# Issuing the K, V and G mixing products together in three row groups, with a new order on every engine, in an attention and mixture-of-experts kernel

## The reference, cut to what matters

```python
shifted = jnp.pad(h, ((0, 0), (1, 0), (0, 0)))[:, :T_]
delta = shifted - h
x1 = jnp.tanh(x0).reshape(B_, T_, 5, R)              # R = 32
x2 = jnp.einsum('btnr,hnr->btnh', x1, x_out_w.reshape(H_, 5, R))
mus = x2 + x_bias
r_mu, w_mu, k_mu, v_mu, g_mu = (mus[:, :, i] for i in range(5))
...
k = (h + delta * k_mu) @ k_w.T
v = (h + delta * v_mu) @ v_w.T
g = (h + delta * g_mu) @ g_w.T
```

## Time and profile before

| | us |
|---|---|
| median of 3 executions | 884.71 (884.67 to 891.51) |
| profiled execution, its own time | 889.28 |
| its span in the trace | 887.3 |
| TensorE busy in the span | 788.1 (89%) |
| GpSimd busy | 552.4 (62%) |
| ScalarE busy | 484.1 (55%) |
| VectorE busy | 471.9 (53%) |

### The profile page before, as it was taken

How to read it: one execution, slowest core, us unless ns; L and a number is a source line. 1 busy time by engine, 2 the same in 40 slices (tenths; PEclk the granted TensorE clock), 3 DMA queues, 4 the chain that set the end, 5 groups by cost and what they waited for, 6 DMA issues and landing times.

```text
span 887.3 us, 24076 instructions
## 1 busy us (share of the span) xinstructions
PE 788.1 (89%) x8042; PEld 569.7 (64%) x8043; DVE 471.9 (53%) x1381; ACT 484.1 (55%) x1147; POOL 552.4 (62%) x691
## 2 busy tenths in 40 slices
PE   4788899999999999999977759999999999999492
PEld 1354455555665656555555449999999999988340
DVE  2435877777777777687754523333333333223076
ACT  2344666656656656566643306666666666546247
POOL 5435678878887888788876634555555555455344
PEclk9977999999999999999999969999999999999796
DMA  4000112202221122211113521222222222222394
GB/s 165 13 26 2 44 54 64 64 24 62 57 67 43 43 59 63 61 41 48 47 41 91 210 69 45 73 71 67 72 70 65 66 66 62 63 61 52 113 314 142
DMA packets 70324, 63.44 MB, mean 71 GB/s; under 512 B 8002, under 2 KB 61640, under 8 KB 70112
## 3 DMA queue, kind: packets, MB, share of 16 engines
q1 hardware_dynamic: 60816, 44.99, 17.9%
q0 software_dynamic: 9152, 17.07, 5.9%
q10 hardware_dynamic: 272, 0.26, 0.1%
HBM read 38.75 MB, written 25.50 MB: 72 GB/s over the span
## 4 chain that ended last, share of the span: by engine, by line
PE 72%; POOL 8%; issue 7%; DVE 4%; ACT 3%; DMA 2%; another core or an unknown queue 2%; SPq 0%; POOLq 0%; ACTq 0%; DVEq 0%
PE psO L616 16%; PE psB L605 15%; PE psO L541 6%; PE psP L332 5%; PE psB L485 4%; POOL w_ring L939 3%; PE psB L443 3%; POOL dispatched_rows L959 3%; PE psP L407 2%; PE psP L323 2%; PE psO L548 2%; PE psP L596 2%; PE psB L475 2%; PE psP L347 2%
## 5 line engine op out<-in xcount | busy, mean ns | idle before, releaser
L982 POOL DMA_INDIRECT expert_results<-yw_all,rows x158 | 155.5, 984 | 155.8 <-ACT yw_all L857 126.9
L616 PEld LDWEIGHTS psO<-w_sb,hide 128*128 128x128 f32 x1264 | 152.9, 192 | 6.7 <-issue 2.9
L616 PE MATMUL psO<-w_sb,hide 128*128 x1264 | 154.5, 275 | 1.0 <-ACT hide L849 1.0
L849 ACT ACTIVATE hide<-psB,w_ring 128x256 f32<-128x256 f32 x316 | 123.8, 475 | 56.0 <-PE psB L605 53.8
L959 POOL DMA_INDIRECT dispatched_rows<-rows,slot x128 | 130.8, 1022 | 35.0 <-issue 31.0
L605 PE MATMUL psB<-x1T,w_ring 128*128 128x256 f32 x632 | 151.3, 383 | 0.6 <-DVE x1T L1283 0.3
L1296 DVE TENSOR_TENSOR K<-psO,b_sb 128x256 f32<-128x256 f32 x79 | 33.6, 425 | 171.4 <-PE psO L616 138.2
L605 PEld LDWEIGHTS psB<-x1T,w_ring 128*128 128x128 f32 x632 | 114.9, 192 | 14.4 <-issue 1.7
L939 POOL TENSOR_TENSOR w_ring<-w_ring,tot 128x128 f32<-128x128 f32 (+2 forms) x160 | 117.9, 759 | 0.0
L857 ACT ACTIVATE yw_all<-K,rows 128x128 f32<-128x128 f32 x158 | 54.8, 395 | 78.5 <-issue 47.1
L1034 DVE SCALAR_TENSOR_TENSOR psP<-psP,cols,delta 128x512 f32<-128x512 f32 x80 | 57.3, 754 | 72.2 <-PE psP L332 72.2
(11 more groups left out here) (172 smaller groups left out, 1302.0 us busy)
## 6 DMA issues: line engine op xcount, KB each, us to landing
rows<-dispatched_rows SPq DMA_DIRECT2D x80, 132.0 KB
w_sb<-expert_results SPq DMA_DIRECT2D x8, 1024.0 KB, 11.9
h_res<-in_hidden SPq DMA_DIRECT2D x16, 256.0 KB, 3.0
out<-w_sb SPq DMA_DIRECT2D x16, 256.0 KB, 2.3
hT<-in_hidden_t SPq DMA_DIRECT2D x15, 256.0 KB, 4.5
w_sb<-in_w SPq DMA_DIRECT2D x14, 256.0 KB
expert_results<-yw_all,rows POOLq DMA_INDIRECT x158
dispatched_rows<-pad_rows SPq DMA_DIRECT2D x17, 132.0 KB
```

The lines of the kernel that those rows point to most:

```text
L616: last = mm(psO[:, p, s * 128:(s + 1) * 128], hide[p][:, c, s * 128:(s + 1) * 128], w2_sb[:, bass.ds(e, 1), c, :].rearrange("p e c -> p (e ...
L849: last = A(hide[p][:, c, :], psB[:, 2 * p + c // 2, (c % 2) * ST:(c % 2 + 1) * ST], ACT.Relu, bias=w1b[i % W_RING][:, HIDDEN + c:HIDDEN + ...
L982: G.indirect_dma_start(back_dram[:, :], bass.IndirectOffsetOnAxis(row_in[i][:, s, AT_DEST:AT_DEST + 1].bitcast(u32), 0), yw[i][:, s, :], N ...
```

## The change

Mixture G's product goes from its own place behind `a_k` to the group of K and V. The three are then issued one after another in row groups 2, 3 and 0, into banks P0, P1 and O1, in place of P0 and P1 with G following in P1 once V's mixture had been read. As O1 is the shared expert's bank, two waits are added: the group waits for `base_out` of the unit four back, and `f_up` 0 waits for `mixed4` (G's mixture) of the unit three ahead. `a_g` now waits for `mixed3` as well, since it writes P1 where V's mixture was. The numbers of products, vector operations and DMAs stay as they were. The order tables of all four engines are new, and the pipeline runs one step more, because the tables count from another unit.

```diff
-MIX_BANK = {MIX_W: 0, MIX_R: 1, MIX_K: 0, MIX_V: 1, MIX_G: 1}
+        mix_in = {MIX_W: P0, MIX_R: P1, MIX_K: P0, MIX_V: P1, MIX_G: O1}
...
-            def a_mix_k_v(u):
+            def a_mix_k_v_g(u):
                 done(pe, "exp_w", u)
                 done(pe, "r_done", u)
-                pe.nop(nofuse=True)
-                mix(P0, MIX_K)
-                mix(P1, MIX_V)
+                before(pe, "base_out", u, 4)
+                pe.nop(nofuse=True)
+                for n in (MIX_K, MIX_V, MIX_G):
+                    mix(mix_in[n], n)
...
-            def a_mix_g(u):
-                done(pe, f"mixed{MIX_V}", u)
-                mix(P1, MIX_G)
...
             def a_g(u):
+                done(pe, f"mixed{MIX_V}", u)
                 done(pe, f"mixed{MIX_G}", u)
...
                     done(pe, "x1T", u)
                     before(pe, "base_out", u)
+                    done(pe, f"mixed{MIX_G}", min(u + 3, UNITS - 1))
...
-                at(2, b_k_tok)
-                at(3, a_mix_k_v)
-                at(2, b_kv)
...
+                at(-1, b_k_tok)
+                at(-2, c_attn)
+                at(0, a_k)
+                at(-1, b_kv)
+                at(-3, f_up, 0)
+                at(0, a_g)
+                at(-1, b_o_far)
+                at(0, a_v)
```

More of the change, by code:

```diff
@@ L218, in pipeline @@
         def pipeline(body):
-            for i in range(-4, UNITS + 3):
+            for i in range(-4, UNITS + 4):
                 def at(d, op, *args):
@@ L367, in a_mix_w_r @@
                 pe.nop(nofuse=True)
-                mix(P0, MIX_W)
-                mix(P1, MIX_R)
+                mix(mix_in[MIX_W], MIX_W)
+                mix(mix_in[MIX_R], MIX_R)
             def a_decay_hid(u):
@@ L553, in body @@
             def body(at):
-                at(0, f_up, 0)
-                at(2, b_o_near)
-                at(2, b_k_tok)
-                at(3, a_mix_k_v)
-                at(2, b_kv)
-                at(0, f_up, 1)
-                at(0, c_place)
-                at(3, a_k)
-                at(3, a_mix_g)
-                at(3, a_v)
-                at(0, f_up, 2)
-                at(2, b_o_far)
-                at(3, a_g)
-                at(1, c_attn)
-                at(3, b_level, 1)
-                at(3, b_level, 0)
-                at(4, a_adapt0)
-                at(0, f_up, 3)
-                at(4, a_adapt1)
-                at(3, b_level, 2)
-                at(0, f_down, 0)
-                at(4, a_mix_w_r)
-                at(3, b_level, 3)
-                at(0, f_down, 1)
-                at(1, c_turn)
-                at(4, a_decay_hid)
-                at(4, a_r)
-                at(1, c_logits)
-                at(3, b_level, 4)
-                at(4, a_w)
+                at(-1, b_o_near)
+                at(-1, b_k_tok)
[6 more added lines that the diff above has]
+                at(0, a_v)
+                at(0, b_level, 1)
+                at(1, a_adapt0)
+                at(-3, f_up, 1)
+                at(0, b_level, 0)
+                at(1, a_adapt1)
+                at(-3, f_up, 2)
+                at(-2, c_turn)
+                at(0, b_level, 2)
+                at(1, a_mix_w_r)
+                at(-3, f_up, 3)
+                at(-2, c_logits)
+                at(0, b_level, 3)
+                at(-3, f_down, 0)
+                at(1, a_decay_hid)
+                at(1, a_r)
+                at(-3, f_down, 1)
+                at(1, a_w)
+                at(-2, c_place)
+                at(0, b_level, 4)
+                at(1, a_mix_k_v_g)
             pipeline(body)
@@ L814, in body @@
             def body(at):
-                at(0, b_o)
-                at(1, a_g)
-                at(1, a_v)
-                at(2, a_adapt0)
-                at(-2, f_hid, 3)
-                at(2, a_adapt1a)
-                at(2, a_adapt1b)
-                at(-1, c_x1)
-                at(0, c_sq)
-                at(-1, c_x1T)
-                at(2, a_decay_hid)
-                at(-1, c_logits)
-                at(2, a_r)
-                at(2, a_w)
-                at(-1, f_hid, 0)
-                at(1, b_k_tok)
-                at(1, b_chunk_decay)
-                at(2, a_r_near)
-                at(-1, f_hid, 1)
-                at(2, a_k)
-                at(-1, c_rows1)
-                at(2, a_k_near)
-                at(2, a_decay)
-                at(-1, c_top_exp)
-                at(0, c_aff)
-                at(-1, f_hid, 2)
+                at(3, a_decay)
+                at(0, f_hid, 0)
+                at(3, a_g)
+                at(2, b_o)
+                at(2, c_sq)
+                at(3, a_v)
+                at(4, a_adapt0)
+                at(0, f_hid, 1)
+                at(1, c_x1)
+                at(4, a_adapt1b)
+                at(4, a_adapt1a)
+                at(0, f_hid, 2)
+                at(1, c_x1T)
+                at(0, f_hid, 3)
+                at(1, c_logits)
+                at(4, a_decay_hid)
+                at(4, a_r)
+                at(1, c_top_exp)
+                at(4, a_w)
+                at(2, c_aff)
+                at(3, b_k_tok)
+                at(4, a_r_near)
+                at(3, b_chunk_decay)
+                at(4, a_k)
+                at(1, c_rows1)
+                at(4, a_k_near)
             pipeline(body)
```

90 lines of the change are left out of this document (45 added, 45 removed).

## The result

| | before | after |
|---|---|---|
| median, same chip | 888.11 us (884.67 to 892.12, 4 runs) | 991.81 us (984.03 to 998.2, 4 runs) |
| profiled execution | 889.28 us | 992.62 us |
| from one `b_o_far` to the next, mean of 11 units | 28.4 us | 35.4 us |

The kernel became slower by a factor of 1.116 (95% interval 1.106 to 1.126), 104 us. The forecast was 896 us, with a range to 906.

What follows compares the result with a forecast made beforehand. TensorE was taken as the bound (busy 27.06 of 28.40 us), GpSimd second. Cycle 27.6, with late signals 28.6, plus clock falls 0.6: 29.2 us, +0.9; twelve units add 11 to 884.7, giving 896 us, range 871 to 906.

Steps and rivals of the forecast that it cites:

- Three row groups side by side: TensorE's mixing products K, V, G run together, saving 1.06 us a unit; the rival that they don't had chance 0.03.
- The new wait in front of `a_g`: TensorE waits for V's mixture, now last on VectorE: `a_g` starts 5.4 us after `b_k_tok`, idle 1.4 us every unit.
- The cycle: Way from `b_k_tok` through `a_g`, the levels and GpSimd's steps to the next `b_k_tok`: 27.6 us with signals on time.
- GpSimd's 27.0 us: GpSimd's list without its waits for TensorE, claimed as the floor no unit can go below: about 27.0 us.
- Late signals: TensorE's signals beside GpSimd's scatters arrive about 1.2 us late, lengthening the unit from 27.6 to 28.6 us.
- only `b_kv` late: Case where only `b_kv`'s signal is late: the scan starts at 4.2 instead of 3.4 us, the unit takes 28.4 us.
- The clock: TensorE's clock falls to half behind the hole before `a_g` in one of two units: 0.57 us a unit.
- never less: Claim that more TensorE idle time in one piece makes clock falls more frequent, never less; bounds one in three and each.
- Signals on time: Rival, chance 0.25: lateness belongs to the old order's place, not the scatters; unit 28.0 to 28.2 us, 881 to 883 us.
- Every unit slowed: Rival, chance 0.12: K's signal late (28.8 us) and a clock fall in each unit: 29.9 us, 904 up to 908 us.
- GpSimd becomes the bound: Rival, chance 0.20: pieces overlap better, the unit drops to GpSimd's 27.0 us, kernel faster at 869 or 873 us.
- The rest: Other new waits (`base_out`, `mixed4`), the long power, SP's queue, the first stage's start and end, later stages: all cost nothing.

Runs made afterwards that it cites:

- no scatters: Changed kernel with GpSimd's 128 indirect scatters replaced by memsets of about equal length, routed rows not dispatched: 877.35 us on A, 882.04 us on B.
- A: Not a run: the chips on which the kernel before took 885 to 888 us (chips 2 and 4 by the numbers on record).
- the old order without scatters: Kernel before the change with the same memsets in place of the scatters, routed rows not dispatched: 851.37 and 849.69 us on B.
- V first: Changed kernel with V's mixture on VectorE moved ahead of G's, `c_z` and the scan: 909.94 us (1.026) on A, 868.88 us (1.011) on B.
- B: Not a run: the chips on which the kernel before took 859 to 862 us (chips 0 and 5 by the numbers on record).
- scan behind V with one pair moved: Changed kernel with VectorE order K, G, V, `c_z`, scan, and the last scatter pair put behind `b_step` 0: 878.74 us (1.019) on B.
- one pair moved: Changed kernel with the last of GpSimd's scatter pairs put behind `b_step` 0: 937.44 us (1.058) on A, 890.27 us (1.033) on B.
- K first: V first, and on TensorE `a_k` and `b_kv` put ahead of `c_attn`: 930.77 us (1.047) on A.
- the two VectorE orders: Changed kernel with V's mixture ahead of `c_z` and the scan, before G's (909.94 us, 1.026) or behind G's (925.51 us, 1.044), on A.
- `f_up` 0 three times: Changed kernel with the products of `f_up` 0 issued three times into the same bank, as useless work in the hole: 975.16 us (1.100) on A.

## Why the prediction was wrong, step by step

The direction was right and the size was off by 96 us. My cycle has four pieces, and the runs measured each, once without late signals and once with:

| piece | my sum, on time | no scatters, A | after, A |
|---|---|---|---|
| `b_k_tok` to `a_g` | 5.4 | 5.43 | 8.30 |
| `a_g` to `b_level` 1 | 3.64 | 3.83 | 7.14 |
| `b_level` 1 to `b_level` 2 | 5.98 | 5.91 | 6.48 |
| `b_level` 2 to the next `b_k_tok` | 12.6 | 12.33 | 13.41 |
| unit | 27.6 | 27.50 | 35.33 |

**Three row groups side by side: right.** Three products take 1.14 us. The Trainium skill ("TensorE: Matmul & The Clock Gate", section on why this matters for kernels) gave a speedup of 3.07 for four, from which I had estimated up to 1.46 us; the trace is better than that. With or without the grouping the time is the same within 1%.

**The new wait in front of `a_g`: right in place, kind and on-time size.** I had 5.4 us and a hole of 1.4; without scatters it was 5.43 and 1.30.

**The cycle: right in size, partly by luck.** 27.6 against 27.50. But my last piece went through GpSimd's list and counted two holes of 0.68 us behind scatters as if they belonged to signals on time. They were late signals already. Without scatters they are gone, and GpSimd waits for TensorE's `b_level` 4 (0.89 us) instead; 12.6 against 12.33 came out of two errors that cancel. For the same reason GpSimd's 27.0 us was no floor: the old order without scatters took 26.2 us a unit, and V first 27.4 on B.

**What I compared it with: wrong.** I set 27.6, with signals on time, against 27.96, where they were late. With signals on time on both sides it is 27.5 against 26.2: the new wait costs 1.3 us a unit even then, which with a later start is the 31 us of the two kernels without scatters.

**Late signals: the step that failed.** I took 28.6, 1.0 us above the cycle, from the one late signal I had followed, K's (1.2 us), and added it at whichever product stood beside the scatters. K's was now 0.2 us late and `b_kv`'s 3.1. Even for "only `b_kv` late" I let the scan start at 4.2 us behind `b_k_tok`; it started at 6.1 (323.10 - 317.02). `a_g` starts at 8.30: +1.9 us over the 6.4 that is in the forecast of 28.6 (with K late by the full 1.2 it would have been 6.6). `b_level` 3's and 4's signals are late beside their pairs as well: 13.41 against 12.6, +0.8.

**The clock: the term that was mis-sized with it.** I allowed 0.57 us a unit, one fall of 1.14 in two units, a price read behind a hole of 0.75 us. Behind a hole of 4.1 us there was one in each unit, and it covered 8.5 us: 7.14 against 3.64 and 6.48 against 5.98, 4.0 us, or +3.4. The price was already low for the old kernel: its slowed units took 29.25 to 29.43 us beside 27.9, 1.4 and not 1.14. And "never less" doesn't hold: a hole of 1.3 us without scatters was followed by a fall in one unit of eleven, one of 0.75 before in one of three.

1.9 + 0.8 + 3.4 = 6.1 us is the whole difference between my 29.2 and the 35.3 of this unit. Over thirteen units it is 79 us. The ends of the stage, for which I took 0, were 13 (104 - 91), and the kernel before was measured 3.4 us higher this time.

**The rivals.** "Signals on time" had a price of 881 to 883 us; without scatters it was 877 on A. But that takes the scatters away from the new order alone, and the lateness did belong to the scatters, not to the place alone. "Every unit slowed" named the right kind of mechanism (late signal and a fall in each unit), with K late in place of `b_kv` and with the price of the old rows, 904 to 908. "GpSimd becomes the bound" never came near: `a_g` started within 4.8 us of `b_k_tok` in no run with V's mixture behind the scan, and where it did (4.25 us, scan behind V with one pair moved), the unit was still 27.7. **The rest** held, but for the ends.

**Shown and not shown.** That the loss hangs on the scatters (no scatters), on what stands beside which of them (one pair moved, K first) and on V's place behind the scan (the two VectorE orders) is shown. That the hole in front of `a_g` has a part in the clock's falls is shown by `f_up` 0 three times; its length alone doesn't tell how often they come. The unaltered changed kernel on B, and the old order without scatters on A, were not run. How the chip holds a signal back, and why B doesn't, stays open.

## What to carry to other kernels

A delay seen at one instruction is a sample of a mechanism, not its size: before pricing it elsewhere, look at all late signals in the trace (`b_level` 3's was already 2.0 us late before, all but 0.7 of it hidden behind the scatters), since the delay changed from 1.1 to 3.1 us with the place beside four scatters. And look at what the delayed engine has queued behind the wait: with the same 3.1 us the kernel was 102 us slower than before with V's mixture behind the scan and 22 with it ahead. A hole on TensorE can be paid twice, once as a hole and once in the clock of the work behind it, so useless products in it can make a kernel faster (15 us here). And a price of signals on time has to be set against the old kernel with signals on time, not against its measured unit.
